# Summing one-hot matmuls in a graph layer: the matmul of zeros that opens each quad is replaced by a first tile whose one-hots span all 510 columns

## What is computed

```python
seg = dst * NUM_REL + edge_type
xs = x[src]
sums = jax.ops.segment_sum(xs, seg, num_segments=N * NUM_REL)
cnt = jax.ops.segment_sum(jnp.ones(seg.shape, x.dtype), seg, num_segments=N * NUM_REL)
mean = (sums / jnp.maximum(cnt, 1.0)[:, None]).reshape(N, NUM_REL, -1)
return jnp.einsum('nrd,rdo->no', mean, w_rel) + x @ root + bias
```

## Time and profile before

| | |
|---|---|
| median of 3 runs | 4824.44 us (4823.83 to 4830.43) |
| the profiled execution: its time | 4821.75 us |
| its span, first to last instruction | 4819.8 us |
| PE busy | 2410.4 us, 50% |
| DVE busy | 2126.7 us, 44% |
| POOL busy | 2969.1 us, 62% |
| mean granted TensorE clock | 0.684 |

### The profile page before, as it was taken

One profiled execution on the slowest core, in us unless ns is written; L12 is line 12 of the kernel. 1 busy time (PEld: TensorE's weight loads), 2 busy tenths in 40 slices (PEclk: granted clock), 3 DMA queues, 4 the chain that ended last, 5 costly groups with the idle time before them and its releaser, 6 DMA issues.

```text
span 4819.8 us, 58181 instructions
## 1 busy us (share of the span) xinstructions
PE 2410.4 (50%) x13845; PEld 2126.7 (44%) x13846; DVE 2126.7 (44%) x3980; ACT 979.0 (20%) x3133; POOL 2969.1 (62%) x3140
## 2 busy tenths in 40 slices
PE   2555555555555556555633545434444454444445
PEld 2444445445454455545533434333334443343444
DVE  5444545444444445444533434433343343343435
ACT  0222212112222222222211222212221222221223
POOL 6666666666666666666546666666666666666663
PEclk6676767666666667667766667766766666676667
DMA  4222222222222222222111211212221121212111
GB/s 101 65 59 63 64 62 62 62 63 63 59 65 64 59 63 63 63 62 63 44 35 51 54 52 52 53 51 54 53 53 53 51 54 53 53 53 54 52 53 36
DMA packets 206632, 275.68 MB, mean 57 GB/s; under 512 B 62732, under 2 KB 156428, under 8 KB 206444
## 3 DMA queue, kind: packets, MB, share of 16 engines
q0 software_dynamic: 100032, 205.07, 16.4%
q1 hardware_dynamic: 101534, 67.96, 5.0%
q10 hardware_dynamic: 4878, 0.86, 0.2%
HBM read 260.85 MB, written 12.80 MB: 57 GB/s over the span
## 4 chain that ended last, share of the span: by engine, by line
another core or an unknown queue 37%; issue 22%; DVE 18%; PE 17%; DVEq 5%; ACT 1%; DMA 0%; SPq 0%; ACTq 0%
PE ps_agg L1599 10%; DVE z_s L1899 5%; DVE ring L1856 4%; DVE S L1830 3%; PE ps_agg L1595 3%; DVEq L1834 2%; PE ps_y L1625 2%; PE ps_cnt L1584 1%; DVEq L1855 1%; ACT prod L1504 1%; DVE hit L1821 1%; DVE cnt_ring L1847 1%; DVE amax L1793 1%; DVEq L1856 1%
## 5 line engine op out<-in xcount | busy, mean ns | idle before, releaser
L1306 POOL DMA_INDIRECT rows<-table,idx_s x1563 | 1475.0, 944 | 902.3 <-issue 573.9
L1306 POOL DMA_INDIRECT rows<-in_x_dram,idx_s x1507 | 1431.3, 950 | 875.3 <-issue 463.1
L1856 DVE TENSOR_TENSOR ring<-ps_agg,ring 128x510 f32 x784 | 539.7, 688 | 2231.7 <-remote 1805.5
L1599 PE MATMUL ps_agg<-S,rows 128*128 128x140 f32 x6272 | 1297.1, 363 | 219.7 <-issue 217.5
L1599 PEld LDWEIGHTS ps_agg<-S,rows 128*128 128x128 f32 x6272 | 1248.8, 264 | 289.5 <-issue 241.3
L1595 PE MATMUL ps_agg<-zero_b 128*128 128x510 bf16 x784 | 402.4, 513 | 1056.4 <-DVE ring L1856 715.9
L1625 PE MATMUL ps_y<-wall,ring 128*128 128x128 f32 x3920 | 646.6, 309 | 549.4 <-issue 546.3
L1625 PEld LDWEIGHTS ps_y<-wall,ring 128*128 128x128 f32 x3920 | 579.4, 221 | 569.2 <-issue 566.2
L1504 ACT ACTIVATE prod<-ps_y,rc_s 128x128 f32<-128x128 f32 x1960 | 542.5, 381 | 1228.8 <-remote 814.2
L1595 PEld LDWEIGHTS ps_agg<-zero_b 128*128 128x128 bf16 x784 | 87.8, 112 | 1162.5 <-DVE ring L1856 665.2
L1899 DVE TENSOR_REDUCE z_s<-prod 128x128 f32<-128x1536 f32 (+1 forms) x196 | 564.9, 2882 | 15.4 <-ACT prod L1507 14.6
(11 more groups left out here) (111 smaller groups left out, 1050.6 us busy)
## 6 DMA issues: line engine op xcount, KB each, us to landing
attr<-in_edge_attr_dram SPq DMA_DIRECT2D x97, 336.0 KB
rows<-table,idx_s POOLq DMA_INDIRECT x1563
rows<-in_x_dram,idx_s POOLq DMA_INDIRECT x1507
x_in<-in_x_dram SPq DMA_DIRECT2D x97, 64.0 KB
table<-h_s SPq DMA_DIRECT2D x97, 64.0 KB
x_in<-table SPq DMA_DIRECT2D x97, 64.0 KB
prod<-in_x_dram SPq DMA_DIRECT2D x97, 64.0 KB
out_dram<-o_s SPq DMA_DIRECT2D x97, 64.0 KB
```

The costliest lines, as they stand in the source:

```text
L1306: pool.indirect_dma_start(out=rows[:, slot, j, :], out_offset=None, in_=(x, htab)[l][:, :], in_offset=bass.IndirectOffsetOnAxis(ap=at, axi ...
L1599: ins = t_.matmul(ps_agg[h][:, bass.ds(off[j] * R, TCOL)], lhsT=rows[:, o % PER, j, :], rhs=S[:, o % 2, j, :], start=False, stop=(c == 3))
L1856: v_.tensor_tensor(win, ps_agg[h][:, 0:QCOL].rearrange("p (n r) -> p r n", r=R), win, ALU.add).then_inc(agg_taken, 1)
```

## The change

The matmul of zeros goes. In its place the quad's first tile has one-hots over all 510 columns of the bank, its matmul starts the sum and so writes the whole bank, and only the other three tiles have 140 columns at an offset (the first tile's offset is 0 by construction). S is laid out anew: per quad 510 columns and then three times 140, so 1860 columns an oct in place of 1120. DVE makes them with three instructions in place of one: the two first tiles together (1020 columns), then the three other tiles of each quad (420 columns each). The row of column numbers `ps_iota` is made 510 long, once, at the start.

```diff
-        S = sb("S", [P, 2, GT, TCOL])
+        S = sb("S", [P, 2, 2 * SQ])
...
                     for h in range(2):
                         pe.wait_ge(agg_taken, g * 2 + (h + 1))
-                        t_.matmul(ps_agg[h][:, 0:QCOL], lhsT=zero_b[:, 0:P], rhs=zero_b[:, 0:QCOL],
-                                  start=True, stop=False)
-                        for c in range(4):
-                            j = 4 * h + c
+                        t_.matmul(ps_agg[h][:, 0:QCOL], lhsT=rows[:, o % PER, 4 * h, :],
+                                  rhs=S[:, o % 2, h * SQ:h * SQ + QCOL], start=True, stop=False)
+                        for c in range(1, 4):
+                            j, at = 4 * h + c, h * SQ + QCOL + (c - 1) * TCOL
                             ins = t_.matmul(ps_agg[h][:, bass.ds(off[j] * R, TCOL)], lhsT=rows[:, o % PER, j, :],
-                                            rhs=S[:, o % 2, j, :], start=False, stop=(c == 3))
+                                            rhs=S[:, o % 2, at:at + TCOL], start=False, stop=(c == 3))
                         ins.then_inc(agg_ready, 1)
...
-            link(v_.tensor_copy(ps_iota[:, 0:TCOL], iota_c[:, :]))
+            for m in range(0, QCOL, TCOL):
+                n = min(TCOL, QCOL - m)
+                link(v_.tensor_scalar(ps_iota[:, m:m + n], iota_c[:, 0:n], float(m), None, ALU.add))
...
-                    v_.tensor_tensor(S[:, sl, :, :], bc1(ps_iota[:, 0:TCOL], GT, TCOL),
-                                     bc(comb_t[:, bass.ds(g * GT, GT)], GT, TCOL), ALU.is_equal).then_inc(S_ready, 1)
+                    comb = comb_t[:, bass.ds(g * GT, GT)].rearrange("p (q c) -> p q c", c=4)
+                    hot = S[:, sl, :].rearrange("p (q w) -> p q w", q=2)
+                    v_.tensor_tensor(hot[:, :, 0:QCOL], bc1(ps_iota[:, 0:QCOL], 2, QCOL),
+                                     comb[:, :, 0:1].to_broadcast([P, 2, QCOL]), ALU.is_equal)
+                    for h in range(2):
+                        ins = v_.tensor_tensor(hot[:, h, QCOL:SQ].rearrange("p (c w) -> p c w", w=TCOL),
+                                               bc1(ps_iota[:, 0:TCOL], 3, TCOL), bc(comb[:, h, 1:4], 3, TCOL),
+                                               ALU.is_equal)
+                    ins.then_inc(S_ready, 1)
```

More of the change, by code:

```diff
@@ L1087 @@
 QCOL = QWIN * R
+SQ = QCOL + 3 * TCOL
 RN = PER * P
@@ L1704, in _ @@
                              ALU.subtract).then_inc(nat_ready, 1)
-            rising = S[:, :, :, :].rearrange("p a j c -> p (a j c)")[:, 0:CHUNKS * (P - 1)]
+            rising = S[:, :, :].rearrange("p a c -> p (a c)")[:, 0:CHUNKS * (P - 1)]
             rising = rising.rearrange("p (k c) -> p k c", k=CHUNKS)
             link(v_.tensor_tensor(rising, nat_d[:, :, 1:P], nat_d[:, :, 0:P - 1], ALU.is_ge))
-            link(v_.tensor_reduce(out=sorted_p[:, 0:1], in_=S[:, :, :, :].rearrange("p a j c -> p (a j c)")
+            link(v_.tensor_reduce(out=sorted_p[:, 0:1], in_=S[:, :, :].rearrange("p a c -> p (a c)")
                                   [:, 0:CHUNKS * (P - 1)], op=ALU.min, axis=AX.X))
```

## The result

The changed kernel took 4837.06 us in the median (4829.7 to 4847.84), the kernel before 4824.27 us in the same comparison: ratio 1.003, 95% interval 1.0022 to 1.0039. That is +12.8 us, slower by 0.3%. I had forecast +2.5%; the number belongs to the rival "hidden in the loops, paid only at the ends". All ratios here are of fast runs; one of e2's eleven runs, at 5626 us, is left out of them.

A forecast was written before the change was run, and what follows sets the result against it. POOL's gathers were taken as pacemaker, held up by the chain of PE, DVE and ACT. Loops +128, ends +21, 25 given back: +124 us on 4821.75, so 4946, rounded to 4945 us (+2.5%); range 4680 to 5230.

The forecast's parts named there:

- hidden in the loops, paid only at the ends: Rival: PE's crawl ends when POOL pauses, so longer bursts eat dead time alone; 4845 us, chance 0.20.
- The bound: Loops: POOL's gathers set the pace; dead time of PE, DVE and ACT, about 12 us each two steps, delays them.
- PE's term: PE's quads: longer fp32 opener in place of the zeros, +0.68 us a quad, +1.36 an oct, 533 us in all.
- DVE's term: DVE's making of S: three instructions, 2.41 us for 1.32, +1.09 us an oct, 427 us in all.
- a quarter of PE's part: Loops: 0.25 of PE's 1.36 us reaches the end, 0.34 us an oct, 128 us, from comparing the two passes.
- The cover is the crawl: a longer burst leaves less of it: Loops: PE's crawl, one instruction per 0.7 us between bursts, hides added work, but longer bursts shrink it.
- The ends: Between the passes and behind the last gather: 25 quads pay PE's 0.55 us and half DVE's part, 0.27; 21 us.
- The 25 us given back: Loops: 2352 fewer PE instructions, some 5% in the crawl at 0.7 us each, 80 us, a quarter counted: 25 us.
- The faster one: Rival: the chain is bound by issue, so fewer PE instructions make the crawl later or shorter; 4640 us, chance 0.24.
- Work on the path in full: Rival: POOL waits for each oct, +1.36 us an oct; 5355 us, or 5780 with DVE in series; chance 0.12.

The follow-up runs named there:

- e2: Kernel before with DVE's part alone: new layout of S made with three DVE instructions, PE still opening with the zeros; 4834.2 us, 1.0022.
- e9: The kernel before, unchanged, traced on a chip of the faster kind; 4428.01 us in its one run.
- e3: Changed kernel with the old form in the last lap of each pass; 1.0006 of the kernel before.
- e14: Changed kernel with the first tile's 510-column matmul issued four times, on a chip of the slower kind; 5050.01 us, 1.0356 of the kernel before.
- e1: Kernel before with PE's part alone: 510-column fp32 opener in place of the zeros, S and DVE as before; 4827.61 us, 1.0014.
- e6: Changed kernel with POOL gathering four tiles of each oct, not eight; 3115.26 us, against 2916.58 for the kernel before with the same halving.
- e15: Kernel before without POOL's waits for landed rows, on a chip of the slower kind; 5136.76 us, 1.0545 of the kernel before.
- e10: The changed kernel, unchanged, on a chip of the faster kind; 4421.72 us, 0.9997 of the kernel before.
- e13: Changed kernel with the first tile's 510-column matmul issued twice, on a chip of the faster kind; 4425.81 us, 1.0000 of the kernel before.
- e17: Changed kernel with the first tile's 510-column matmul issued three times, on a chip of the faster kind; 4430.69 us, 1.0023 of the kernel before.

## Why the prediction was wrong, step by step

**The bound.** POOL as pacemaker with PE's dead time behind the rest was right. That the dead time belongs to the chip, or to its state, and not to the kernel I could not see in one trace; e9 shows it.

**PE's term, +0.68 us a quad, 533 us.** The price of the work held. PE in order of time in the changed kernel, a quad at the low clock and the start of the next:

```profile
1458.97 2.06 PE L1596 MATMUL ps_agg<-S,rows 128*128 128x510 f32 x2
1460.83 1.61 PE L1600 MATMUL ps_agg<-S,rows 128*128 128x140 f32 x6
1462.23 1.68 PE L1596 MATMUL ps_agg<-S,rows 128*128 128x510 f32 x2
```

From quad to quad that is 3.26 us, where I had 3.11, for 2.27 before; at full clock the medians are 1.66 and 1.18. Of the two openers the second takes the 0.85 and 0.43 us forecast, the first 1.01 and 0.45. The mix of the clock's levels didn't hold. By the clock record and the start of each quad, of the quads that lie wholly at one level 54% were at the low one before (I had 62%), and 29% after. At an unchanged 54% the change would cost 0.54 x 0.99 + 0.46 x 0.48 = +0.76 us a quad. Measured as busy time (opener and all other matmuls) a quad went from (402.4 + 1297.1)/784 = 2.17 us to (1118.6 + 876.1)/784 = 2.54 us, +0.38, and PE's other matmuls became shorter too (the transform 646.6 us before, 576.7 after), so that PE as a whole is busy 203.8 us more, and 7.35 and 5.90 us an oct in the loops in place of my 8.3 and 6.7. The granted clock rose from 0.684 to 0.735, and that took about half of the quads' term away. I had put the clock at what it was before the change.

**DVE's term, +1.09 us an oct.** Nearly right: 475.7 + 426.1 in place of 516.1 is +0.98 us an oct, with 1.213 and 0.584 us where I had 1.21 and 0.60.

**The step that failed: "a quarter of PE's part", 0.34 us an oct, 128 us.** The loops paid nothing: 1237 gathers for 1240, 1148 for 1146, and e3, with 93% of the octs changed, 1.0006. I had read the 0.39 us between the loops of the two passes as the price of 1.57 us of PE work. It isn't that. Where slow stretches are absent the two loops take the same time: in e9 1211 gathers in 1700 us and 1286 in 1800, 11.23 and 11.20 us an oct, with the same difference in matmuls (41 and 29.5 an oct) and in DVE's work (5.95 and 4.68 us), if a smaller one in PE's busy time (6.58 and 5.85). And where they are present 4.2 us of PE work an oct cost little: e14 is 176 - 13 = 163 us slower than the changed kernel, 35 of them at the ends (83.9 and 77.2 us in place of 71.5 and 54.2), which leaves 128/378 = 0.34 us an oct in the loops. My rule gives that price to 1.4 us of work. (An estimate, since the two kernels ran on different chips of the kind.) "The cover is the crawl: a longer burst leaves less of it" is the reason that failed with it: most crawls end with POOL's pause, wherever PE is by then. What does make pass 1 slower on such a chip isn't settled; it also has 41 matmuls an oct for 29 (6378/155, 4219/143.3), and more transfers (62 GB/s for 53).

**The ends, 21 us.** Right in kind and place, 13.7 in size: 7.4 us on 12 quads and 6.3 on 13, 0.55 a quad for PE's and DVE's part together. Here my split was off: e1 and e2 give 5 us to PE's part and 8 to DVE's, where I had 14 and 7.

**The 25 us given back.** Nothing supports it: e1, which has the fewer PE instructions without DVE's part, isn't faster but 0.14% slower.

**The rivals.** The faster one is ended by e1 as well. Work on the path in full is what e6 shows, at 0.74 of PE's added time (or 0.58 of DVE's), but only with POOL's gathers halved. The hidden one held, and so did its reason, "The crawl ends when POOL pauses, whatever PE has done before; then longer bursts eat dead time alone": 441 of 561 slow stretches end in a pause, at a steady lag, whatever their length, and in e15 the index waits double when the landing waits go. I had given it 0.20, less than half of the forecast's chance, though the earlier trace rows already showed one such end. My range of 4680 to 5230 us holds the 4837 measured only because it was drawn round the rivals as well; the forecast's own 4885 to 5075 doesn't.

"Runtime: NRT & Kernel Launch" of the Trainium skill, in its section on instruction fetch, lets straight-line code stream in nearly for free. In e9 the trace agrees: 20 matmuls in 2.77 us. On the chips at 4820 us it doesn't, at 0.7 us an instruction; that it is fetching which is late there was not measured.

## What to carry to other kernels

Ask of an engine that is half idle whether the idle time is elastic, and which event ends it. Two loops of one kernel with different work are no measure of the price of work, unless the rest of them is alike; a dose that is raised until it shows (free with two, 0.2% with three, 3.6% with four on the other kind of chip) is one. Look for the cost of hidden work where its cover stops: ahead of a barrier and behind the last transfer.

A version that beats both kernels here is the kernel before without POOL's landing waits: 3976 us, 10% faster, on two chips, but 5.5% slower on a third. A tuning result that hangs on waits between gathers should be timed on more than one chip.

## What the runs showed of the hardware that I had not expected

Two kinds of chip, or of its state: the kernel before takes 4420 to 4426 us on three of them and 4820 to 4875 us on two others, on each within 0.4%. The slower kind shows PE at one instruction in 0.7 us for about 12 us of each two steps while POOL gathers, and puts 29 to 45% of the chain (9% in e14) down to "another core or an unknown queue"; the faster kind shows neither. What makes the difference isn't in the profile.

Of 561 slow stretches of PE in the eight traces 441 end while POOL pauses, in the median of each trace 2.8 to 3.1 us behind its last gather: what ends them goes with POOL's indirect gathers and not with PE's own work.

The granted clock followed PE's load, on the faster kind 0.728, 0.764, 0.858 and 0.917 for PE busy 55, 64, 72 and 83% of the span (e9, e10, e13, e17): added PE work came partly free because all of it ran faster. A mean over the span hides at which level the work runs: in e9, at 0.728, 97% of the quads that lie wholly at one level are at the low one.
